# A one-core routed-experts block on one NeuronCore: two PSUM banks for the experts' sums, part of the modulations on ScalarE and GpSimd, and a new written order of all steps

## What is computed

```python
mod = (silu(c) @ wmod).reshape(8, 6, 1, -1)
sa, ca, ga, sb, cb, gb = (mod[:, k] for k in range(6))
ga = (2 * (ga >= 0) - 1) * maximum(abs(ga), 0.25)          # gb in the same way
h = layernorm(x) * (1 + ca) + sa
x = x + ga * attn(h)     # attn, for each sequence:
#   scores = relu(h @ w1 + b1) @ w2 + b2;  the 128 best rows are taken, in their order
#   n1 = ln(tok); u, res = n1 @ m_in_w; u = u * conv_w + conv_b
#   y = u * (Bv.sum * Cv) * silu(res);  tok = tok + y @ m_out_w
#   n2 = ln(tok); gate = top 2 of 8 experts
#   tok += sum_e gate_e * (gelu(n2 @ moe_w1[e] + b1[e]) @ moe_w2[e] + b2[e]);  tok *= softmax weight
h = layernorm(x) * (1 + cb) + sb                            # feed-forward part, on all rows
q = fp4_quant_dequant
y = q(silu(q(h) @ q(w_gate).T) * (q(h) @ q(w_up).T)) @ q(w_down).T
out = x + gb * y
```

## Time and profile before

| | |
|---|---|
| median of 3 runs | 245.74 us |
| the profiled execution's own time | 245.69 us |
| its span | 243.9 us |
| TensorE busy (matmul) | 218.0 us, 89% |
| TensorE weight loads (beside the matmuls) | 176.6 us, 72% |
| VectorE busy | 200.7 us, 82% |
| ScalarE busy | 131.7 us, 54% |
| GpSimd busy | 72.6 us, 30% |
| mean granted TensorE clock | 0.987 |

### The profile page before, as it was taken

How to read it: one execution, slowest core, us unless ns; L and a number is a source line. 1 busy time by engine, 2 the same in 40 slices (tenths; PEclk the granted TensorE clock), 3 DMA queues, 4 the chain that set the end, 5 groups by cost and what they waited for, 6 DMA issues and landing times.

```text
span 243.9 us, 4519 instructions
## 1 busy us (share of the span) xinstructions
PE 218.0 (89%) x1431; PEld 176.6 (72%) x1436; DVE 200.7 (82%) x667; ACT 131.7 (54%) x343; POOL 72.6 (30%) x92
## 2 busy tenths in 40 slices
PE   2999889799999999999898999989989999998770
PEld 0345566588877899788785788878978997896540
DVE  3699998958998899887779999885997999988860
ACT  2124386999828753453776465517434757462320
POOL 7112102710353014423031201030036125662861
PEclk9999999979999999999999999999999999999997
DMA  5699590100010000000000000000000000000100
GB/s 154 173 335 364 213 344 0 48 22 0 0 35 23 0 3 11 13 0 23 4 1 11 0 3 1 3 0 0 0 0 15 11 4 22 13 32 0 34 33 22
DMA packets 9126, 12.01 MB, mean 49 GB/s; under 512 B 1184, under 2 KB 5256, under 8 KB 9104
## 3 DMA queue, kind: packets, MB, share of 16 engines
q1 hardware_dynamic: 8080, 9.63, 12.2%
q0 software_dynamic: 1024, 2.10, 2.9%
HBM read 10.65 MB, written 1.07 MB: 48 GB/s over the span
## 4 chain that ended last, share of the span: by engine, by line
DVE 40%; PE 32%; issue 11%; ACT 8%; POOL 4%; DMA 3%; SPq 1%; DVEq 0%; ACTq 0%; POOLq 0%
PE down_ps L1076 14%; PE up_ps L1076 9%; PE aux_ps L1076 8%; DVE acc L993 4%; DVE q_am L760 3%; DVE stats L730 3%; DVE qa L773 3%; POOL rstd L505 2%; ACT perm_m L604 2%; DMA wmod_s<-wmod_dram 2%; ACT h1T L669 2%; DVE hx L836 2%; DVE hh L1049 2%; DVE hh L1045 2%; DVE hx L829 2%
## 5 line engine op out<-in xcount | busy, mean ns | idle before, releaser
L669 ACT ACTIVATE h1T<-up_ps,par 128x256 f32<-128x256 f32 (+1 forms) x160 | 58.1, 434 | 40.8 <-PE up_ps L1076 32.6
L1076 PE MATMUL down_ps<-w_s,h1T 128*128 128x128 f32 x512 | 67.8, 280 | 5.2 <-DVE acc L993 4.3
L1076 PEld LDWEIGHTS down_ps<-w_s,h1T 128*128 128x128 f32 x512 | 63.5, 194 | 11.8 <-issue 9.9
L1076 PE MATMUL up_ps<-n2T,w_s 128*128 128x256 f32 (+1 forms) x320 | 66.3, 342 | 2.0 <-ACT h1T L669 2.0
L1076 PEld LDWEIGHTS up_ps<-n2T,w_s 128*128 128x128 f32 x320 | 49.7, 192 | 8.8 <-issue 4.9
L505 POOL TENSOR_TENSOR rstd<-veps,half_pow 128x2 f32<-128x2 f32 (+3 forms) x17 | 14.9, 875 | 83.9 <-DVE veps L735 83.9
L993 DVE SCALAR_TENSOR_TENSOR acc<-down_ps,gate,acc 128x128 f32<-128x128 f32 x64 | 20.2, 346 | 8.6 <-PE down_ps L1076 8.0
L1076 PE MATMUL aux_ps<-w_guT,h2T 128*128 128x352 f32 x64 | 21.4, 460 | 0.0
L1076 PE MATMUL up_ps<-lower,ones_b 128*128 128x512 bf16 x76 | 18.9, 379 | 0.5 <-issue 0.3
L558 ACT ACTIVATE qb<-qa 128x704 f32<-128x704 f32 (+5 forms) x20 | 11.3, 569 | 14.3 <-DVE qa L764 14.3
L543 POOL DMA_INDIRECT out_dram<-yo,row_ix x16 | 16.2, 1011 | 5.4 <-issue 2.4
(11 more groups left out here) (188 smaller groups left out, 339.7 us busy)
## 6 DMA issues: line engine op xcount, KB each, us to landing
w_s<-moe_w_dram SPq DMA_DIRECT2D x16, 256.0 KB, 5.6
mod_r<-mod_dram SPq DMA_DIRECT2D x1, 2048.0 KB, 7.5
mod_r<-mod_dram SPq DMA_DIRECT2D x1, 768.0 KB, 4.7
...
```

The lines of the kernel that those rows point to most:

```text
L669: last = A.activation(h1T[:, m % 2, hc, 0:n], up_ps[j % UP_BANKS][:, h * n:(h + 1) * n], ACT.Gelu, bias=col("moe_b1", e * HC + hc))
L1076: return nc.tensor.matmul(o, lhsT=l, rhs=r, start=start, stop=stop)
```

## The change

Three things change together.

1. `DOWN_BANKS = 2` and `AUX_BANKS = 4`: the experts' sums alternate between two banks, so the products of an expert wait for the `acc` of the expert two before; all other products share four banks.
2. `mod.0.1`: its copy out of PSUM goes from VectorE to ScalarE, and its arithmetic goes from VectorE (nine instructions on 8x128, four of them fused) to GpSimd (eleven instructions, with a wait between each and the next of a chain).
3. All four tables of order are new. Their steps are the same ones, but for `mod.0.1` and the spare products: 81 before, 52 now.

The diff, with one line of the tables for each side:

```diff
@@ -54,69 +54,68 @@
 UP_BANKS = 2
-AUX_BANKS = 5
+DOWN_BANKS = 2
+AUX_BANKS = 4
...
-modh.0.0 mod.0.0-1 modh.0.1 spare.23.0 hT.0.0 spare.3.1 hr.0.0 wT.0.0 spare.1.2 srow.0.0 spare.4.3 scol.0.0
+modh.0.0-1 mod.0.0 hT.0.0 hr.0.0 srow.0.0 wT.0.0 scol.0.0 mod.0.1 spare.9.0 hT.1.0 place.0.0 hr.1.0 spare.2.1
...
@@ -276,7 +275,7 @@
         mod_t = spare[0:B, NMOD * D:(NMOD + 2) * D].rearrange("p (k d) -> p k d", d=D)
 
         up_ps = [ps(f"up_ps{i}", [P, 512]) for i in range(UP_BANKS)]
-        down_ps = ps("down_ps", [P, MAXB, D])
+        down_ps = [ps(f"down_ps{i}", [P, MAXB, D]) for i in range(DOWN_BANKS)]
         aux_ps = [ps(f"aux_ps{i}", [P, 512]) for i in range(AUX_BANKS)]
 
         ld_par, ld_wmod_a, ld_wmod_b, ld_attn, ld_ffn = (
@@ -289,6 +288,7 @@
         c_tanh_ready = sem("c_tanh_ready")
         silu_c_ready = sem("silu_c_ready")
         mod_ready = sem("mod_ready")
+        mod_step = sem("mod_step")
         mod_stored = [sem(f"mod_stored{i}") for i in range(2)]
         mod_rows = [sem(f"mod_rows{i}") for i in range(2)]
         bc_ready = sem("bc_ready")
@@ -523,6 +523,27 @@
                         out=xp[:, b0 + k, half, :], out_offset=None, in_=x[:, :],
                         in_offset=bass.IndirectOffsetOnAxis(ap=row_ix[:, c:c + 1], axis=0)
                     ).then_inc(gathered[a][half], 16)
+                elif kind == "mod":
+                    wait_aux_taken(pool, kind, a, i, 0)
+                    step_no = 0
+                    v = mod_s[:, CB * D:(CB + 1) * D]
+                    nc.gpsimd.tensor_scalar(v, v, 1.0, None, ALU.add)
+                    for m in (GA, GB):
+                        v, sign, size = mod_s[:, m * D:(m + 1) * D], mod_t[:, 0, :], mod_t[:, 1, :]
+                        nc.gpsimd.tensor_scalar(sign, v, 0.0, 2.0, ALU.is_ge, ALU.mult).then_inc(mod_step, 1)
+                        pool.wait_ge(mod_step, step_no + 1)
+                        nc.gpsimd.tensor_scalar(sign, sign, -1.0, None, ALU.add).then_inc(mod_step, 1)
+                        pool.wait_ge(mod_step, step_no + 2)
+                        nc.gpsimd.tensor_tensor(size, sign, v, ALU.mult).then_inc(mod_step, 1)
+                        pool.wait_ge(mod_step, step_no + 3)
+                        nc.gpsimd.tensor_scalar(size, size, 0.25, None, ALU.max).then_inc(mod_step, 1)
+                        pool.wait_ge(mod_step, step_no + 4)
+                        last = nc.gpsimd.tensor_tensor(v, sign, size, ALU.mult)
+                        if m == GA:
+                            last.then_inc(mod_step, 1)
+                            pool.wait_ge(mod_step, step_no + 5)
+                            step_no += 5
+                    last.then_inc(mod_ready, 1)
                 elif kind in ("wqs", "fqs", "hqs"):
                     pool.wait_ge(qr_ready, N_QR[(kind[0:2] + "b", a, i)])
                     wait_buffer_free(pool, kind[0:2], a, i)
@@ -567,6 +588,10 @@
                     A.activation(mod_r[:, i, SA, :], aux(kind, a, i, 0)[:, 0:D], ACT.Copy)
                     A.activation(mod_r[:, i, CA, :], aux(kind, a, i, 0)[:, D:2 * D], ACT.Identity,
                                  bias=ones[:, 0:1]).then_inc(aux_taken(kind, a, i, 0), 1)
+                elif kind == "mod":
+                    wait_aux_full(act, kind, a, i, 0)
+                    A.activation(mod_s[:, GA * D:], aux(kind, a, i, 0)[0:B, :], ACT.Copy
+                                 ).then_inc(aux_taken(kind, a, i, 0), 1)
                 elif kind == "wT":
                     wait_aux_full(act, kind, a, i, 0)
                     act.wait_ge(ld_par, 16)
@@ -797,24 +822,9 @@
                 elif kind == "mod":
                     src = aux(kind, a, i, 0)
                     wait_aux_full(dve, kind, a, i, 0)
-                    if i == 0:
-                        V.tensor_copy(mod_s[:, 0:D], src[0:B, 0:D])
-                        V.tensor_scalar(mod_s[:, D:2 * D], src[0:B, D:2 * D], 1.0, None, ALU.add
-                                        ).then_inc(aux_taken(kind, a, i, 0), 1)
-                    else:
-                        V.tensor_copy(mod_s[:, GA * D:], src[0:B, :]).then_inc(aux_taken(kind, a, i, 0), 1)
-                        wait_aux_taken(dve, kind, a, i, 0)
-                        v = mod_s[:, CB * D:(CB + 1) * D]
-                        V.tensor_scalar(v, v, 1.0, None, ALU.add)
-                        for m in (GA, GB):
-                            v = mod_s[:, m * D:(m + 1) * D]
-                            V.tensor_scalar(mod_t[:, 0, :], v, 0.0, 2.0, ALU.is_ge, ALU.mult)
-                            link(V.scalar_tensor_tensor(mod_t[:, 1, :], v, -1.0, v, ALU.mult, ALU.max))
-                            link(V.tensor_scalar(mod_t[:, 1, :], mod_t[:, 1, :], 0.25, None, ALU.max))
-                            last = V.scalar_tensor_tensor(v, mod_t[:, 0, :], -1.0, mod_t[:, 1, :], ALU.add, ALU.mult)
-                            if m == GA:
-                                link(last)
-                        last.then_inc(mod_ready, 1)
+                    V.tensor_copy(mod_s[:, 0:D], src[0:B, 0:D])
+                    V.tensor_scalar(mod_s[:, D:2 * D], src[0:B, D:2 * D], 1.0, None, ALU.add
+                                    ).then_inc(aux_taken(kind, a, i, 0), 1)
                 elif kind == "lnA":
                     dve.wait_ge(ld_x[a], 16)
                     moments(LN[("h", a)], lambda t: hx[:, c0 + t, 0:D], ch)
@@ -990,7 +1000,7 @@
                     dve.wait_ge(down_full, m + 1)
                     for t in range(tiles):
                         b = first + t
-                        last = V.scalar_tensor_tensor(acc[:, b, :], down_ps[:, t, :], gate[:, b, i:i + 1], acc[:, b, :],
+                        last = V.scalar_tensor_tensor(acc[:, b, :], down_ps[m % DOWN_BANKS][:, t, :], gate[:, b, i:i + 1], acc[:, b, :],
                                                       ALU.mult, ALU.add)
                     last.then_inc(down_done, 1)
                     dve.wait_ge(down_done, m + 1)
@@ -1226,10 +1236,10 @@
                     if t == 0:
                         pe.wait_ge(ld_w2[e], 16)
                         pe.wait_ge(up_done, N_UPDONE[("gelu", a, (e + 1) * HC // per_bank(a) - 1)])
-                        if m > 0:
-                            pe.wait_ge(down_done, m)
+                        if m >= DOWN_BANKS:
+                            pe.wait_ge(down_done, m - DOWN_BANKS + 1)
                     for hc in range(HC):
-                        last = mm(down_ps[:, t, :], h1T[:, m % 2, hc, t * P:(t + 1) * P], w2_s[:, e, hc, :],
+                        last = mm(down_ps[m % DOWN_BANKS][:, t, :], h1T[:, m % 2, hc, t * P:(t + 1) * P], w2_s[:, e, hc, :],
                                   hc == 0, hc == HC - 1)
                     if t == tiles - 1:
                         last.then_inc(down_full, 1)
```

More of the change, by code:

```diff
@@ new lines @@
+srow.1.0 perm.0.0-1 scol.1.0 spare.13.2 n1.0.0 spare.1.3 place.1.0 inproj.0.0 wM.0.0 inproj.0.1-2 perm.1.0
+inproj.0.3 perm.1.1 mix.0.0 attn.0.0 n1.1.0 spare.3.4 mix.1.0 inproj.1.0-2 n2.0.0 inproj.1.3 up.0.0-1 logits.0.0
+up.0.2 down.0.0 up.0.3 down.0.1 attn.1.0 up.0.4-5 down.0.2 gateT.0.0 down.0.3 bias2.0.0 up.0.6 wqT.0.0 hT.2.0
+up.0.7 down.0.4 up.0.8 down.0.5 up.0.9 n2.1.0 hT.2.1 down.0.6-7 up.0.10-11 down.0.8 wqT.0.1 logits.1.0 up.0.12
+hr.2.0 down.0.9 wqT.0.2 up.0.13 down.0.10-11 up.0.14 gateT.1.0 up.0.15 down.0.12 srow.2.0 up.1.0 down.0.13
@@ L79 @@
+down.4.5 gu.6.0 up.4.7 down.4.6 dn.4.0 down.4.7 hqT.4.1 hqT.5.0 spare.2.5 dn.4.1 spare.6.6 h2T.7.0 spare.1.7
+gu.7.0 dn.5.0 hqT.6.0 spare.12.8 dn.6.0 hqT.7.0 spare.3.9 dn.7.0
 """
 DVE_ORDER = """
-silu.0.0 lnA.0.0 mod.0.0-1 lnB.0.0 wbc.0.0 lnC.0.0 lnA.1.0 lnB.1.0 lnA.2.0 scol.0.0 wM.0.0 rank.0.0 lnC.1.0
-pl.0.0 lnB.2.0 n1A.0.0 lnC.2.0 n1B.0.0 scol.1.0 lnC.2.1 mix.0.0 rank.1.0 yA.0.0-1 yB.0.0 pl.1.0 attn.0.0 n2A.0.0
-n1A.1.0 n2B.0.0 n1B.1.0 ix.0.0 smA.0.0 ix.1.0 scol.2.0 ix.0.1 mix.1.0 rank.2.0 lgA.0.0 smA.1.0 yA.1.0 pl.2.0
@@ L95 @@
-yo.7.0
+silu.0.0 lnA.0.0 mod.0.0 lnB.0.0 lnC.0.0 lnA.2.0 lnA.1.0 lnB.1.0 scol.0.0 lnC.1.0 rank.0.0 pl.0.0 wq.0.0 ix.0.0
+n1A.0.0 scol.1.0 n1B.0.0 rank.1.0 wbc.0.0 pl.1.0 yA.0.0 ix.0.1 wM.0.0 yA.0.1 n1A.1.0 yB.0.0 mix.0.0 n1B.1.0
+attn.0.0 n2A.0.0 ix.1.0 mix.1.0 n2B.0.0 yA.1.0 lnB.2.0 yA.1.1 yB.1.0 lnC.2.0 lgA.0.0 ix.1.1 wq.0.1 lgB.0.0
+smA.0.0 wqb.0.0 attn.1.0 n2A.1.0 wqb.0.1 bias2.0.0 n2B.1.0 acc.0.0-1 lnC.2.1 wq.0.2 smA.1.0 fin.0.0 acc.0.2
+wqb.0.2 acc.0.3 lgA.1.0 fq.0.0 lgB.1.0 acc.0.4 fin.2.0 acc.0.5 smB.0.0 acc.0.6 fqb.0.0 scol.2.0 rank.2.0 acc.0.7
@@ L120 @@
+rsf.7.0 out.4.0-1 out.5.0 out.6.0 out.7.0
 """
```

79 lines of the change are left out of this document (34 added, 45 removed).

## The result

The changed kernel takes 253.95 us (median of 4 runs, 252.97 to 255.22) against 245.84 for the kernel before (245.6 to 247.86) in the same session: a ratio of 1.031, 95% interval [1.0262, 1.0358]. It is 3% slower. I had forecast 242.0.

What follows compares the result with a forecast made beforehand. TensorE was taken to set the pace, with VectorE at 86% close behind. Head +0.3, middle +2.1 - 0.5 - 1.9 - 2.8, tail -0.9 sum to -3.7 us: from 245.69 to 242.0 us, bounds 240.3 to 243.6.

Steps and rivals of the forecast that it cites:

- The step that failed first: Head: `mod.0.1` on GpSimd takes 4.1 us, ends near 28, costs 0; without cover 1 to 2 us.
- +4 for the head: Head: upper bound on its +0.3 us, for a clock low until the first `up`.
- The head's other steps: Head: `lnC.0.0` ends near 10.6, half-speed products follow, nine spare products delay the chain, first `up` at 42.4; +0.3 us.
- The inference on the clock after the idle start: Head: TensorE, idle from 7.75 to 10.6, then runs at half speed, costing 1.6 us more on four steps.
- the term of the second bank: Middle: a second bank for the experts' sums removes two thirds of TensorE's 4.3 us of `acc` waits; -2.8 us.
- the forecast -3.1: Middle, from first `up` to `acc.4.7`: the total change forecast, in us.
- -1.9 for the clock at the first activation: Middle: an earlier first activation keeps TensorE's idle time short, so the half-speed stretch there goes; -1.9 us.
- the sign that I named: Middle: no granted clock of 0.50 after 49 us would show the forecast right.
- The condition that I set: Middle, first activation: the clock isn't lost if TensorE's idle time stays under 2 us.
- The tail: After the last `down`: -0.9 us, from -0.5 at `acc.4.7`, -0.7 at `hqb.6.0` and +0.3 for `yo.5.0`.
- Slower by the fourth bank: Rival, chance 0.15: products miss a bank at 0.39 us a wait; ten waits eat the gain, fourteen give 247.3.
- Low clock up to the first `up`: Rival, chance 0.12: the head runs at low clock until the first `up`; 244.5 to 246.2 us.

Runs made afterwards that it cites:

- experiments 1: Changed kernel with the root of the first norm (`rs1.0.0`) moved ahead of `mod.0.1` in GpSimd's order: 248.27 us, ratio 1.0115 to the kernel before.
- 9: Kernel of experiment 8 with the root of the first norm put back behind `mod.0.1` and `gather.0.0`: 247.9 us, ratio 1.0056 to the kernel before.
- experiment 6: Kernel of experiment 1 with `acc.3.0` moved ahead of `fin.5.0` and `acc.4.1` ahead of `hq.4.1`: 245.06 us, ratio 0.9944 to the kernel before.
- 7: Kernel of experiment 1 with 20 more spare TensorE products in the head: 245.58 us, ratio 0.9988 to the kernel before.
- experiment 8: Kernel of experiment 6 with experiment 7's spare products in the head and 8 more in the tail: 242.05 us, ratio 0.9831 to the kernel before.

## Why the prediction was wrong

**The step that failed first** is this one of the head: "It ends near 28, and what waits is `gather.0.0` and then `rs1.0.0` ... So I cost it at 0; without that cover it is 1 to 2 us." Two things were wrong with it. The size: 11 x 0.37 = 4.1 us from a row of another instruction of GpSimd, measured 7.2 (6.8 in the kernels where the root goes first). And the cover: I wrote that the root is wanted only after `scol.1.0` at 29.5, which is right (VectorE was ready at 29.95), and set against it an end of `mod.0.1` near 28; with the gather (1.23 us) and the root (0.74) behind it, the root's end came to 30.0 even so, and there was no slack for an error of 3 us. The bound for a lost cover should have been the whole queue, 7.2 + 1.2 + 0.7 us and 0.3 between them from 23.66, that is 33.1, less 29.95: nearly all of the 3.2 us that VectorE waited. With the low clock behind it this is 4.8 to 5.5 us by the ratios of experiments 1 and 9. The prediction's +4 for the head was for a low clock that starts with the idle start and lasts; it had no term for a wait that brings the clock down again.

**The head's other steps held.** With the root ahead the first `up` is at 42.28 in the fastest run (forecast 42.4) and at 43.83 in experiment 6; the end of `lnC.0.0` is 9.20 + 1.14 = 10.34 (forecast 10.6); `hr.0.0` at half speed, 1.07 us for four pieces where the next group's take 0.63; the nine spare products hold up the chain. The inference on the clock after the idle start is confirmed. With more spare products the first `up` comes at 40.90, 1.4 us before that of the fastest run without them.

**The middle: the term of the second bank.** "The order of before needs VectorE ahead of its load by up to 4 us at a `down`, the new one at most 2.2 ... -2.8 us." The waits fell from 11 places to 3 but grew from 4.3 to 5.3 us: 1.14 at `down.0.4`, for which I had 0.5, and 2.29 and 1.85 at two places for which I had none. My sum along the orders took each step at its usual duration, and priced VectorE's conflict with GpSimd at one step only, `wq.0.0`. But all three waits stand behind VectorE instructions that lasted too long beside a GpSimd product, with no idle time of VectorE between them and the sum that is late. In front of the first, `n2B.1.0` took 1.84 us for two instructions of 0.60 and ends (64.58) when GpSimd's product does (64.49):

```profile
62.74 1.84 DVE L771 TENSOR_SCALAR xh<-acc,mv,rstd 128x128 f32<-128x128 f32 x2
```

```profile
63.64 0.85 POOL L411 TENSOR_TENSOR w_gu_s<-qa,q_sc 128x384 f32<-128x384 f32 x1
```

In front of the second it is `fin.5.0`, 1.5 us too long, and in front of the third three short steps between 209.25 and 212.2 (0.92 for 0.17, 0.54 for 0.29, 0.36 for 0.19), 1.2 us together. That is 3.8 of the 5.3 us by these rows, though no run takes away a GpSimd product alone. The other 1.5 us my walk along the orders should have found. The waits then cost the clock too. The middle without a low clock is 178.8 us (experiments 1 and 7) beside 178.4 before, so the forecast -3.1 became +0.4; the changed kernel's profile has 180.6, with two low-clock stretches behind these waits. With the two sums moved the middle is 176.4, -2.1 to before against my -3.1, with the banks and the order in it together. What the second bank by itself brings in the new order stays open: that order can't run with one bank, since by the tables `down.0.2` would wait for `acc.0.0`, which VectorE has behind `bias2.0.0`, whose product TensorE has behind `down.0.3`. So no run separates the bank from the order.

**-1.9 for the clock at the first activation** held at its place: the first activation comes 2.1 us after the first `up` (50.93), where it came 5.8 after it before, TensorE's waits for it and the next are 0.75 and 0.37 us, and no low clock follows them. But the sign that I named, no granted clock of 0.50 after 49 us, failed: it is 0.52 from 185.9 and from 216.3. The condition that I set, idle time under 2 us, isn't safe either, as the stretch at 216.3 follows a wait of 1.85 us. **The tail** gained nothing in the changed kernel: `acc.4.7` starts 0.9 us after the last `down` (at 228.55, where TensorE goes on), 1.1 before, so 0.2 of the 0.5 us came. TensorE waited 2.30 us for the last tokens' codes, 1.62 before, and ran at 0.51 from 237.0 to 240.4. Where the clock stays up there it is 22.9 us, -0.4 against my -0.9. That is so in experiment 8, but also in 6, which hasn't the tail's spare products; so no run shows that they earn anything in a single execution.

**The rivals.** Slower by the fourth bank (0.15): the right sign by another cause. Low clock up to the first `up` (0.12): it came, in two pieces, of which the first (9.7 us) is in the forecast itself and the second (6.8 us) follows the wait for the root, and its bound of 246.2 had no room for that wait. I had no rival in which a moved step blocks the queue it is moved into. That was the missing case, and so was one in which GpSimd's products make VectorE late at a `down`. (Fourteen waits of 0.39 us on top of 242.0 give 247.5, not the 247.3 of the slower rival; nothing hangs on it.)

That the fastest kernel measures 242.05 beside a forecast of 242.0 is no vindication: it has a head 1.7 us shorter than forecast, by spare products that the change doesn't have, and a middle 1.0 us longer, which took two more moves in VectorE's order. That the two numbers agree is luck.
